# Layer 1 attention reordered: two q/k units at steps 4 and 6, the output projection in halves through the single bank, low parts a score tile later

## Chip, cores and metric

One core of one Trainium2 chip. The metric is the device time of one execution in microseconds. The kernel before took 2039.24 us in the median of 3 runs (2036.27 to 2040.58).

## What is computed

Two transformer-like layers on x of 8 batches x 512 tokens x 256 features, each layer being x + attention(layernorm(x)) + ffn(layernorm(x)). The change lies in layer 1's attention alone (16 heads of 16, a bias that depends on the distance of two positions):

```python
qkv = jnp.einsum('bsd,ed->bse', x, Wqkv); q, k, v = jnp.split(qkv, 3, axis=-1)
logits = jnp.einsum('bihd,bjhd->bhij', q, k) * scale + pos_bias[None]
attn = jax.nn.softmax(logits, axis=-1)
out = jnp.einsum('bhij,bjhd->bihd', attn, v).reshape(B, S, D)
return jnp.einsum('bsd,ed->bse', out, Wout)
```

## The kernel before

Layer 1's attention is `biased_attention` (L656 to L1188). All 8 batches run through one software pipeline. A batch has 32 steps (STEPS). Each step issues one score tile (L1118 on PE: two matmuls for two heads, 128 queries x 512 keys; on VectorE, L1042, two passes that add the bias and take the row maximum) and one probability tile (L1136 on PE, 128 keys x 512 queries for two heads), which belongs to a step 12 earlier (LAG). Of four probability tiles three are copied out of PSUM by ScalarE (L991) and get their bias from GpSimd (L950, through `add_bias` L831), and one (n % 4 == 1) gets it from VectorE straight out of PSUM (L1055). ScalarE takes the exponential three steps later (TAKEN, L994), and at every second step PE multiplies two exponentiated tiles with the values ("value", L1147) into o_bank.

High precision products are made of two parts of each operand: ScalarE writes a high part in fp32r, VectorE the rest (the "low part": L1033 for x, L1036 for q and k, L1040 for the mixed heads), and three matmuls of fp32r stand for one (PARTS, `product` L1087).

Everything else that a batch needs is placed at fixed steps (L732 to L751), some of it for the next batch (+1) and some for the last (-1): load and norm of x (x_load, ln_stats, ln_rstd, ln), its transposes (x_turn, steps 18 and 19), the four q/k units of the next batch ("qk", 22, 23, 28, 29: q and k for heads 0 to 7, then q and k for heads 8 to 15), the products for v (17), the transposed maxima ("maxima", 1, 9, 17, 25), the turn and norm of each head quad (heads_turn, heads_norm), the two turns of the last batch's mixed heads (mix_turn, 24 and 27) and its output projection and store ("out", "store", 31). "stack" (steps 27 and 28 for the next batch, 4 and 12 for this one) is six DMAs on SyncE's queue that copy q/k parts into the layout of the score tiles; it waits for both low parts of its half of the heads (L911). "maxima" puts two DMAs on the same queue (L925), and the first probability tile of a quad waits for them (L1141).

The order is one list for all engines (STEADY): for every step the placed events, then prob, prob_exp and score. Each engine walks it (`turns`, L791) and executes its own part in that order, with semaphores between. Turns -1, 0, 7 and 8 are written out; turns 1 to 6 are a hardware loop (L798).

PSUM: three slots of two banks hold the paired uses (score, prob, v, out) in turn; a use waits until the one three places earlier in the list has been read (`claim`, L1073). One single bank holds maxima, x_turn, qk, heads_turn and mix_turn, each waiting for VectorE's last read of the one before. o_bank holds the values' sum. In the opening batch x_turn and qk use the slots instead of the single bank (`bank`, L782).

```python
for s in range(STEPS):
    STEADY += placed[s]
    STEADY.append(("prob", 0 if s >= LAG else -1, (s - LAG) % STEPS))
    at = s - LAG - TAKEN
    STEADY.append(("prob_exp", 0 if at >= 0 else -1, at % STEPS))
    STEADY.append(("score", 0, s))
```

## Time and profile before

| what | value |
|---|---|
| median of 3 runs | 2039.24 us (2036.27 to 2040.58) |
| the profiled execution | 2048.42 us |
| its span, first to last instruction | 2046.7 us |
| mean granted clock of TensorE | 0.930 |
| busy over the span | PE 87%, PEld 56%, DVE 56%, ACT 52%, POOL 48% |
| layer 1 attention, scores | first 1195.37, last 1813.25 us from the start |

```profile
span 2046.7 us, 34076 instructions
...
PE   4988988887999999999996967878878778877999
PEld 3455555544788888888885733333334333326566
DVE  5666566662253353443433368767877877845435
ACT  2455555555532232232322228877877878885642
POOL 2344444432344444434432528766766767784202
PEclk7899999997999999999998959989889888988999
```

PE is TensorE's matmuls, PEld its weight loads, DVE is VectorE, ACT ScalarE, POOL GpSimd, SP SyncE. Each digit is the busy share of a fortieth of the span (51 us) in tenths; PEclk is the clock that was granted, in tenths of 2.4 GHz. Layer 1's attention fills slices 24 to 36. In the rows of a timeline the columns are: start in us, duration in us, engine, line, operation, output<-input, shape, how many instructions are merged, and in brackets the idle time before with the engine and tile that ended it. Matmuls overlap, so a merged row's duration runs to the end of its last one. A score tile on VectorE is two rows of L1049; L1089 is the matmul of `product`, whoever calls it; L835 is the addition of the bias.

### The profile page before, as it was taken

The numbers are of one execution on the slowest core, as the hardware profiler recorded it, in microseconds if no ns is written. First come the engines' busy times: TensorE is split into PE (matmuls) and PEld (weight loads), VectorE is DVE, ScalarE is ACT, GpSimd is POOL, SyncE is SP. The second block draws the span as 40 slices with busy tenths as digits, with TensorE's granted clock in tenths as the row PEclk, the third lists the DMA queues.
The fourth block names the chain that finished last, engine by engine and source line by source line (L and its number), as shares of the span: only waits on it lengthen the run. The fifth ranks groups of instructions, "written<-read, shape, count | busy, mean of one in ns | idle before, by whom it ended". The sixth has DMA issues, their size and how long they took to land. (4 is left out here: it accounts for less than half of the span.)

```text
span 2046.7 us, 34076 instructions
## 1 busy us (share of the span) xinstructions
PE 1773.9 (87%) x11015; PEld 1149.2 (56%) x11015; DVE 1150.4 (56%) x2519; ACT 1066.1 (52%) x1455; POOL 978.8 (48%) x736
## 2 busy tenths in 40 slices
PE   4988988887999999999996967878878778877999
PEld 3455555544788888888885733333334333326566
DVE  5666566662253353443433368767877877845435
ACT  2455555555532232232322228877877878885642
POOL 2344444432344444434432528766766767784202
PEclk7899999997999999999998959989889888988999
DMA  3333333324420121111201442222122222116456
GB/s 120 86 104 101 90 93 89 93 66 148 160 80 24 56 68 35 56 54 38 67 27 55 160 151 78 82 60 79 56 76 90 62 68 77 42 55 228 129 157 209
DMA packets 119261, 182.74 MB, mean 89 GB/s; under 512 B 14197, under 2 KB 73077, under 8 KB 119162
## 3 DMA queue, kind: packets, MB, share of 16 engines
q1 hardware_dynamic: 110076, 171.11, 27.4%
q10 hardware_dynamic: 8448, 8.39, 1.2%
q0 software_dynamic: 640, 2.10, 0.3%
q8 instruction: 42, 0.69, 0.1%
q14 instruction: 55, 0.45, 0.1%
HBM read 90.72 MB, written 39.91 MB: 64 GB/s over the span
## 5 line engine op out<-in xcount | busy, mean ns | idle before, releaser
L835 POOL TENSOR_TENSOR l_prob<-l_prob,l_bias 128x1024 f32<-128x1024 f32 x192 | 452.8, 2378 | 165.0 <-ACT l_prob L991 164.3
L1268 POOL TENSOR_TENSOR f_hl<-f_full,f_hh 128x512 fp32r<-128x512 f32 x192 | 248.4, 1294 | 410.3 <-DVE f_hh L1306 270.5
L1049 DVE CUSTOM_DVE_ANT_0 l_slot<-l_slot,l_bias 128x512 f32<-128x512 f32 x512 | 340.5, 715 | 73.0 <-PE l_slot L1128 62.9
L994 ACT ACTIVATE l_prob<-l_prob 128x1024 f32<-128x1024 f32 x256 | 270.9, 1070 | 0.0
L493 DVE TENSOR_REDUCE l_peak<-l_slot 128x2 f32<-128x256 f32 (+3 forms) x256 | 206.3, 822 | 108.8 <-PE l_slot L585 105.6
L1356 PE MATMUL f_ps<-f_hh,f_hi_h 128*128 128x512 f32 x1024 | 260.3, 390 | 3.4 <-ACT f_hh L1280 2.5
L1356 PE MATMUL f_ps<-f_hl,f_hi_h 128*128 128x512 f32 x1024 | 258.3, 389 | 0.0
L397 ACT ACTIVATE l_prob<-l_slot 128x1024 f32<-128x1024 f32 (+3 forms) x256 | 175.4, 706 | 100.8 <-PE l_slot L604 97.9
L991 ACT COPY l_prob<-l_slot 128x1024 f32<-128x1024 f32 x192 | 194.7, 1014 | 50.1 <-PE l_slot L1144 49.5
L1356 PEld LDWEIGHTS f_ps<-f_hh,f_hi_h 128*128 128x128 f32 x1024 | 192.0, 188 | 46.7 <-issue 3.2
L1356 PEld LDWEIGHTS f_ps<-f_hl,f_hi_h 128*128 128x128 f32 x1024 | 192.2, 188 | 39.9
L1288 ACT ACTIVATE f_full<-f_ps,f_h_s 128x512 f32<-128x512 f32 x128 | 87.0, 685 | 234.8 <-PE f_ps L1356 215.9
L336 POOL TENSOR_SCALAR_AFFINE_SELECT l_prob<-l_prob 128x256 f32<-128x256 f32 x256 | 106.1, 422 | 213.8 <-ACT l_prob L397 211.2
L1306 DVE CAST f_hh<-f_full 128x512 fp32r<-128x512 f32 x128 | 62.2, 486 | 256.2 <-ACT f_full L1288 256.2
L1128 PE MATMUL l_slot<-l_stacks 63*128 63x512 f32 x512 | 125.0, 488 | 61.5 <-DVE l_prob L835 27.4
L1158 PE MATMUL l_o_bank<-l_prob,l_vals 128*32 128x512 f32 x1024 | 155.3, 682 | 4.7 <-ACT l_prob L994 4.7
L1144 PE MATMUL l_slot<-l_stacks 64*128 64x512 f32 x512 | 138.3, 539 | 22.4 <-DVE l_peak L1049 16.2
L1144 PEld LDWEIGHTS l_slot<-l_stacks 64*128 64x128 f32 x512 | 52.8, 204 | 138.7 <-DVE l_peak L1049 85.1
L580 PE MATMUL l_slot<-l_stacks 63*128 63x256 f32 (+2 forms) x512 | 98.8, 383 | 29.8 <-ACT l_prob L397 16.4
L604 PE MATMUL l_slot<-l_stacks 64*128 64x256 f32 (+2 forms) x512 | 111.6, 435 | 11.3 <-DVE l_peak L493 4.1
L1128 PEld LDWEIGHTS l_slot<-l_stacks 63*128 63x128 f32 x512 | 54.4, 209 | 101.1 <-DVE l_prob L835 41.7
L618 PE MATMUL l_o_bank<-l_prob,l_vals 128*32 128x512 f32 (+3 forms) x1024 | 101.5, 470 | 9.9 <-POOL l_prob L336 8.7
(228 smaller groups left out, 2811.7 us busy)
## 6 DMA issues: line engine op xcount, KB each, us to landing
l_stacks<-l_parts SPq DMA_DIRECT2D x384, 128.0 KB, 2.6
attn<-l_out_sb ACTq DMA_DIRECT2D x16, 512.0 KB, 3.1
f_raw<-in_L_ffn_h_w SPq DMA_DIRECT2D x16, 512.0 KB, 4.1
f_raw<-in_L_ffn_h_w SPq DMA_DIRECT2D x32, 256.0 KB, 2.6
e_w<-in_L_ffn_f SPq DMA_DIRECT2D x32, 256.0 KB, 3.0
l_bias<-ext SPq DMA_DIRECT2D x16, 448.0 KB, 8.5
l_x_in<-in_L_attn_x SPq DMA_DIRECT2D x8, 512.0 KB, 3.9
xh<-l_xh SPq DMA_DIRECT2D x8, 512.0 KB, 2.6
```

Source lines behind the costliest of these rows:

```text
L397: act.activation(prob[:, n // 2 % RING, 2 * pr:2 * pr + 2, j * P:T], slot(kind, n)[:, :, j * P - q0:wide], ACT.Exp).then_inc(p_exp.sem, 1)
L493: dve.tensor_reduce(peak[:, g, :, pr, t], slot(kind, n)[:, :, 0:(t + 1) * P], AX_X, ALU.max)\
L604: ins = pe.matmul(out[:, a, 0:wide], stacks[r, 1, 2 * g + pr, j * P:(j + 1) * P], stacks[r, 0, 2 * g + pr, q0:T], start=True, stop=True)
L835: return eng.tensor_tensor(probs(n), src, bias[:, h:h + 2, j * P:j * P + T], ALU.add)
L991: act.copy(probs(n), slot(kind, n)[:]).then_inc(p_copied.sem, 1)
L994: act.activation(probs(n), probs(n), ACT.Exp).then_inc(p_exp.sem, 1)
L1049: ins = dve.tensor_tensor_reduce(src, src, bias[:, 4 * g + 2 * pr + a, t * P:t * P + T], 1.0, 3 * NEG, ALU.add, ALU.max, peak[:, g, a, pr, ...
L1128: ins = pe.matmul(out[:, a], stacks[r, 0, 2 * g + pr, t * P:(t + 1) * P], stacks[r, 1, 2 * g + pr, ::-1], start=True, stop=True)
L1144: ins = pe.matmul(out[:, a], stacks[r, 1, 2 * g + pr, j * P:(j + 1) * P], stacks[r, 0, 2 * g + pr, ::-1], start=True, stop=True)
L1158: ins = pe.matmul(o_bank[32 * a:32 * a + 32, :], vals_sb[:, v0:v0 + 32], prob[:, n % RING, a], start=(j == 0), stop=(j == TT - 1), skip_gr ...
L1268: pool.tensor_tensor(t.hl[layer % 2][:, o], t.full[:, n % 2], t.hh[layer % 2][:, o].bitcast(F32), ALU.subtract).then_inc(self.h_lo.sem, 1)
L1356: ins = pe.matmul(t.hidden[n % 4][:], t.hi[m][:, k, cut], src[layer % 2][:, k], start=first and k == 0, stop=last and k == KH - 1, skip_gr ...
```

## The change

The list of steps is changed, and with it what the single bank and the slots hold.

- q/k units 2 and 3 leave steps 28 and 29 of the batch before; they are computed in their own batch at steps 4 and 6. Unit 1 moves from step 23 to 24, mix_turn 0 from 24 to 23. Stack 2 moves from step 4 to 8.
- The low part of a q/k unit is an event of its own on VectorE, behind the score tile of the step instead of ahead of the additions and the score.
- The output projection is two events (steps 30 and 31) of 12 matmuls each into the single bank, each copied by ScalarE (512 columns); the store follows the second. It no longer takes a slot, so the list of paired uses has 65 entries instead of 66 and its ring of three starts anew at each batch: at the wrap the claim is two uses back instead of three (`claim` looks for the last use of the same slot).
- In the opening batch units 2 and 3 also go through the single bank, and the first score waits for two low parts instead of four.

```diff
--- before.py
+++ after.py
@@ -720,7 +720,7 @@
     value_ps, o_copied, ot_ps = sem("value_ps", QUADS * TT), sem("o_copied", QUADS), sem("ot_ps", QUADS)
     inv_ready, mix_ready = sem("inv_ready", QUADS), sem("mix_ready", QUADS)
     mt_ps, mh_ready, ml_ready = sem("mt_ps", KD), sem("mh_ready", KD), sem("ml_ready", KD)
-    out_ps, out_ready = sem("out_ps", 1), sem("out_ready", 1)
+    out_ps, out_ready = sem("out_ps", TT // 2), sem("out_ready", TT // 2)
     out_saved = sem("out_saved", 1, grant=1, unit=16)
     held_sp, held_dve = sem("held_sp"), sem("held_dve")
 
@@ -737,7 +737,7 @@
         placed[s].append(("heads_copy", off, g))
         off, s = later(8 * g + 9)
         placed[s].append(("maxima", off, g))
-        off, s = later((27, 28, 36, 44)[g] - STEPS)
+        off, s = later((27, 28, 40, 44)[g] - STEPS)
         placed[s].append(("stack", off, g))
     for g, s in enumerate((26, 34, 42, 52)):
         off, s = later(s)
@@ -745,23 +745,25 @@
     for s, *events in ((0, ("x_load", 1, 0)), (17, ("v", 0, 0)),
                        (3, ("ln_stats", 1, 0)), (4, ("ln_stats", 1, 1)), (5, ("ln_stats", 1, 2)),
                        (6, ("ln_stats", 1, 3), ("ln_rstd", 1, 0)), (8, ("ln", 1, 0)),
-                       (18, ("x_turn", 1, 0)), (19, ("x_turn", 1, 1)), (22, ("qk", 1, 0)), (23, ("qk", 1, 1)),
-                       (24, ("mix_turn", -1, 0)), (27, ("mix_turn", -1, 1)), (28, ("qk", 1, 2)), (29, ("qk", 1, 3)),
-                       (31, ("out", -1, 0), ("store", -1, 0))):
+                       (18, ("x_turn", 1, 0)), (19, ("x_turn", 1, 1)), (22, ("qk", 1, 0)), (24, ("qk", 1, 1)),
+                       (4, ("qk", 0, 2)), (6, ("qk", 0, 3)), (23, ("mix_turn", -1, 0)), (27, ("mix_turn", -1, 1)),
+                       (30, ("out", -1, 0)), (31, ("out", -1, 1), ("store", -1, 0))):
         placed[s] += events
     for s in range(STEPS):
         STEADY += placed[s]
+        lows = [("qk_low", off, n) for kind, off, n in placed[s] if kind == "qk"]
         STEADY.append(("prob", 0 if s >= LAG else -1, (s - LAG) % STEPS))
         at = s - LAG - TAKEN
         STEADY.append(("prob_exp", 0 if at >= 0 else -1, at % STEPS))
         STEADY.append(("score", 0, s))
+        STEADY += lows
 
 
     LAST_READ = {"score": a_max, "prob": None, "v": v_ready, "out": out_ready,
                  "maxima": tops_ready, "x_turn": xl_ready, "qk": low_ready, "heads_turn": mix_ready, "mix_turn": ml_ready}
-    PAIRED = [e for e in STEADY if e[0] in ("score", "prob", "v", "out")]
-    SINGLE = [e for e in STEADY if e[0] in ("maxima", "x_turn", "qk", "heads_turn", "mix_turn")]
-    assert len(PAIRED) % 3 == 0
+    PAIRED = [e for e in STEADY if e[0] in ("score", "prob", "v")]
+    SINGLE = [e for e in STEADY if e[0] in ("maxima", "x_turn", "qk", "heads_turn", "mix_turn", "out")]
+    assert len(PAIRED) % 3 != 1
 
     def pooled(n):
         return n % 4 != 1
@@ -781,9 +783,9 @@
 
     def bank(kind, n, b):
 
-        if not opening(b):
+        if not opening(b) or n >= 2:
             return single[:]
-        return slots[2][:, n] if kind == "x_turn" else slots[n // 2][:, n % 2]
+        return slots[2 if kind == "x_turn" else 0][:, n]
 
     def there(b):
         return not isinstance(b, int) or 0 <= b < B
@@ -1000,12 +1002,13 @@
                     wait(act, mt_ps, n + 1, b)
                     act.copy(mixt[:, 0, n], single[:]).then_inc(mh_ready.sem, 1)
                 if kind == "out":
-                    wait(act, out_saved, 1, b - 1)
-                    wait(act, out_ps, 1, b)
-                    act.copy(out_sb[:].rearrange("p (a t) d -> p a (t d)", a=2), slot(kind, 0)[:])\
+                    if n == 0:
+                        wait(act, out_saved, 1, b - 1)
+                    wait(act, out_ps, n + 1, b)
+                    act.copy(out_sb[:, 2 * n:2 * n + 2].rearrange("p t d -> p (t d)"), single[:])\
                        .then_inc(out_ready.sem, 1)
                 if kind == "store":
-                    wait(act, out_ready, 1, b)
+                    wait(act, out_ready, TT // 2, b)
                     act.dma_start(out_d[b].rearrange("(t p) d -> p t d", p=P), out_sb[:]).then_inc(out_saved.sem, 16)
             turns(act, emit)
 
@@ -1031,9 +1034,9 @@
                 if kind == "x_turn":
                     wait(dve, xh_ready, n + 1, b)
                     dve.tensor_tensor(xl[:, n], bank(kind, n, b), xh[:, n].bitcast(F32), ALU.subtract).then_inc(xl_ready.sem, 1)
-                if kind == "qk":
+                if kind == "qk_low":
                     wait(dve, high_ready, n + 1, b)
-                    dve.tensor_tensor(parts[:, n // 2, n % 2 * 3], bank(kind, n, b), parts[:, n // 2, 1 + n % 2].bitcast(F32),
+                    dve.tensor_tensor(parts[:, n // 2, n % 2 * 3], bank("qk", n, b), parts[:, n // 2, 1 + n % 2].bitcast(F32),
                                       ALU.subtract).then_inc(low_ready.sem, 1)
                 if kind == "mix_turn":
                     wait(dve, mh_ready, n + 1, b)
@@ -1073,7 +1076,9 @@
             def claim(uses, depth, kind, n, i):
 
                 at = [(u[0], u[2]) for u in uses].index((kind, n))
-                for m in range(at - depth, at - len(uses) - 1, -depth):
+                for m in range(at - 1, at - len(uses) - 1, -1):
+                    if m % len(uses) % depth != at % depth:
+                        continue
                     before, off, k = uses[m]
                     bb = i + off - (1 if m < 0 else 0)
                     if there(bb):
@@ -1100,7 +1105,7 @@
                 if kind == "qk":
                     if opening(b):
                         pe.wait_ge(w_ready.sem, 2)
-                    else:
+                    if not opening(b) or n >= 2:
                         claim(SINGLE, 1, kind, n, i)
                     weight, cut = (wk if n % 2 else wq), slice(n // 2 * P, (n // 2 + 1) * P)
                     wait(pe, xl_ready, KD, b)
@@ -1119,7 +1124,7 @@
 
                     g, pr, t = score_of(n)
                     if n == 0 and opening(b):
-                        wait(pe, low_ready, 4, b)
+                        wait(pe, low_ready, 2, b)
                     out = claim_pair(kind, n, i)
                     if n % 8 == 0:
                         wait(pe, stack_in[g], 6, b)
@@ -1175,10 +1180,10 @@
                 if kind == "out":
                     if opening(b):
                         pe.wait_ge(w_ready.sem, 4)
-                    out = claim_pair(kind, n, i)
+                    claim(SINGLE, 1, kind, n, i)
                     wait(pe, ml_ready, KD, b)
-                    for t in range(TT):
-                        ins = product(out[:, t // 2, (t % 2) * D:(t % 2 + 1) * D],
+                    for t in range(2 * n, 2 * n + 2):
+                        ins = product(single[:, (t % 2) * D:(t % 2 + 1) * D],
                                       [(mixt[:, q, k, t * P:(t + 1) * P], wo[:, p, k]) for k in range(KD)
                                        for p, q in PARTS])
                     ins.then_inc(out_ps.sem, 1)
```

## Rows read from the trace of the kernel before

**Rows 1.** Busy us by stretch: length, PE, PEld, DVE, ACT, POOL, clock, DMA.
```profile
1505.00:1587.00 82.00, 65.05 (x364) 29.87 (x364) 61.99 (x167) 63.83 (x75) 57.80 (x26) 0.90 0.25 71
```
**Rows 2.** Timeline of VectorE where one batch follows another.
```profile
1504.66 0.70 DVE L1049 CUSTOM_DVE_ANT_0 l_slot<-l_slot,l_bias 128x512 f32<-128x512 f32 x1 [3.01 <-PE l_slot L1128]
...
1582.11 0.70 DVE L1049 CUSTOM_DVE_ANT_0 l_slot<-l_slot,l_bias 128x512 f32<-128x512 f32 x1 [4.36 <-PE l_slot L1128]
...
1586.94 0.70 DVE L1049 CUSTOM_DVE_ANT_0 l_slot<-l_slot,l_bias 128x512 f32<-128x512 f32 x1 [3.43 <-PE l_slot L1128]
...
1749.71 0.70 DVE L1049 CUSTOM_DVE_ANT_0 l_slot<-l_slot,l_bias 128x512 f32<-128x512 f32 x1 [1.09 <-PE l_slot L1128]
```
**Rows 3.** Timeline of PE and VectorE, steps 21 to 25.
```profile
1553.81 0.69 DVE L1049 CUSTOM_DVE_ANT_0 l_slot<-l_slot,l_bias 128x512 f32<-128x512 f32 x1
...
1554.52 0.40 PE L1128 MATMUL l_slot<-l_stacks 63*128 63x512 f32 x2
...
1555.07 0.68 DVE L1036 TENSOR_TENSOR l_parts<-l_single,l_parts 128x512 fp32r<-128x512 f32 x1
...
1555.67 0.69 DVE L1049 CUSTOM_DVE_ANT_0 l_slot<-l_slot,l_bias 128x512 f32<-128x512 f32 x1
...
1555.85 0.50 PE L1089 MATMUL l_single<-l_xl,l_wk 128*128 128x512 f32 x1
...
1557.42 0.50 PE L1144 MATMUL l_slot<-l_stacks 64*128 64x512 f32 x2
...
1558.15 0.69 DVE L1036 TENSOR_TENSOR l_parts<-l_single,l_parts 128x512 fp32r<-128x512 f32 x1 [1.08 <-ACT l_parts L978]
...
1558.89 0.66 PE L1173 MATMUL l_single<-l_ident,l_mix 128*128 128x128 f32 x4 [0.73 <-DVE l_parts L1036]
...
1561.24 0.28 PE L1134 MATMUL l_single<-l_ident,l_peak 128*16 128x128 f32 x1
...
1563.69 0.68 DVE L1049 CUSTOM_DVE_ANT_0 l_slot<-l_slot,l_bias 128x512 f32<-128x512 f32 x1
```
**Rows 4.** Timeline of PE and VectorE, steps 27 to 31.
```profile
1567.62 0.69 DVE L1049 CUSTOM_DVE_ANT_0 l_slot<-l_slot,l_bias 128x512 f32<-128x512 f32 x1
...
1573.92 1.22 DVE L835 TENSOR_TENSOR l_prob<-l_slot,l_bias 128x1024 f32<-128x1024 f32 x1
...
1575.05 0.69 DVE L1049 CUSTOM_DVE_ANT_0 l_slot<-l_slot,l_bias 128x512 f32<-128x512 f32 x1
...
1575.62 1.06 PE L1158 MATMUL l_o_bank<-l_prob,l_vals 128*32 128x512 f32 x8
...
1576.62 4.63 PE L1089 MATMUL l_slot<-l_wo,l_mixt 128*128 128x256 f32 x24
...
1581.51 0.40 PE L1128 MATMUL l_slot<-l_stacks 63*128 63x512 f32 x2
```
**Rows 5.** Busy time by stretch, for PE's granted clock (PEclk).
```profile
1522.60:1532.80 10.20, 7.78 (x32) 3.08 (x28) 6.41 (x17) 8.18 (x11) 6.75 (x4) 0.52 0.02 3
...
1540.80:1543.90 3.10, 3.10 (x30) 2.94 (x26) 0.28 (x3) 1.28 (x2) 3.10 (x2) 1.00 0.12 46
...
1573.80:1577.20 3.40, 2.01 (x13) 0.93 (x14) 3.40 (x9) 2.30 (x3) 1.98 (x1) 0.95 0.54 166
...
1576.60:1581.20 4.60, 4.60 (x30) 4.45 (x26) 1.15 (x4) 0.00 (x0) 1.00 (x1) 0.63 0.00 0
```
**Rows 6.** Busy time by stretch, S4 to S8.
```profile
1513.49:1521.79 8.30, 5.19 (x33) 1.83 (x33) 8.19 (x27) 6.43 (x7) 6.92 (x4) 1.00 0.31 81
```
**Rows 7.** Timeline of SyncE's queue in batch 0.
```profile
1210.19 1.47 SPq L925 DMA_DIRECT2D l_stacks<-l_tops  x2
```
**Rows 8.** Timeline of the end of the attention.
```profile
1845.50 0.63 PE L1173 MATMUL l_single<-l_ident,l_mix 128*128 128x128 f32 x4 [0.90 <-DVE l_mix L1065]
...
1846.78 0.69 DVE L1040 TENSOR_TENSOR l_mixt<-l_single,l_mixt 128x512 fp32r<-128x512 f32 x1 [1.43 <-ACT l_mixt L1001]
...
1854.74 1.01 ACT L1005 COPY l_out_sb<-l_slot 128x1024 f32<-128x1024 f32 x1 [5.47 <-PE l_slot L1089]
```

## Prediction

> **What bounds the kernel now.** I name the score, probability and value tiles S0 to S31, P0 to P31 and V0 to V15; a step issues one S and one P. First view: busy time by stretch. Over one batch of layer 1 attention (82 us) PE is busy 79%, VectorE 76%, ScalarE 78%, GpSimd 70% [rows 1]. No engine is full, so the batch is bound by hand-overs, and the question is where VectorE (which must start an S each step) sits idle. Second view: VectorE's timeline. S0 starts at 1504.66 and at 1586.94, so a batch takes 82.3 us; S31 comes at 1582.11 (VectorE idle 4.36 before it), and S0 follows 4.83 us after S31 [rows 2]. Third view: the same timeline around steps 22 to 31, where two q/k units and the output projection stand. PE runs in order with three paired PSUM slots: anything long put before P and S starves VectorE directly, and a user of the single bank waits until VectorE has read the one before.
>
> **Part 1, steps 22 to 25: low parts later, a mix turn in between.** Per batch the same work, in another order. Before, low 0 starts right after S21 (1555.07), qk1's product runs on PE from 1555.85 to 1557.42 (1.57 us), low 1 follows at 1558.15 after 1.08 us idle, the maxima turn is issued at 1561.24 and S25 starts at 1563.69 [rows 3]. Durations: S takes 1.26 (1553.81 to 1555.07), a low part 0.60 (to 1555.67) and PE goes on 0.74 after its start (1558.15 to 1558.89); PE hands S to VectorE 0.60 after its issue (1581.51 to 1582.11); a mix turn's low part starts 1.28 after the turn (1845.50 to 1846.78) [rows 2, 3, 4, 8].
> Now the new order, from the unchanged issue of S22 at 1554.52. S22 starts at 1555.12, low 0 at 1556.39, and PE gets the bank for the mix turn at 1557.13 (before, qk1 had it at 1555.85). Its low part starts at 1558.41, so S23 at 1559.01, and PE may start qk1 at 1559.15; after 1.57 come P12 and, 0.34 later, S24, issued at 1561.06, started at 1561.66. Low 1 starts at 1562.93. The maxima turn waits for it until 1563.67, 2.4 us later than before; P13 follows 0.2 later, addition 13 starts at 1564.47 and takes 1.13, S25 starts at 1565.60. Cost: 1565.60 - 1563.69 = **+1.91 us**. The chain through the single bank is the path, and each low part behind a score lengthens it by that score. Behind the maxima turn on PE are queued P13, S25 and the heads turn, and VectorE waits for them. Bound from below: +0.6, one low part, if tiles issued ahead covered the rest; from above +2.5, two whole scores. I stay with the chain, since the old rows show no slack in it.
>
> **Part 2, steps 27 to 29: qk2 and qk3 gone.** S27 to S29 took 1575.05 - 1567.62 = 7.43 us: two products of 1.57, each followed by a low part with some 1.1 us of idle before it (as the 1.08 in rows 3), and addition 17, 1.13 until the next starts (1573.92 to 1575.05) [rows 3, 4]. Without them: S27 1.27, S28 1.27 and the addition 1.13 follow without a gap, 3.68 with rounding. Cost: **-3.75 us**. What is late next is ScalarE's copy of P16; it frees S29's slot at about the end of addition 17, so it hides. GpSimd's additions run in 3 of 4 steps and their exponentials are read three steps later: covered. Bound from the other side: -1.5, if only the two idles go and ScalarE's copies set the steps.
>
> **Part 3, the output projection in halves.** Before: 24 matmuls from 1576.62, 4.63 us, then ScalarE's copy of 1.01 us (as in rows 8), the store and only then P19's copy [rows 4]. S29 to S31 is 1582.11 - 1575.05 = 7.06. The size of a half depends on the granted clock. In the projection's stretch it averages 0.63, against 1.00 in the stretch of v, where 24 matmuls of the same width take 3.1 us [rows 5]. The clock fell to 1.2 GHz right after a stretch in which PE was busy 2.01 of 3.40 us, because S29's slot was held by P17 until addition 17 was done [rows 4, 5]. In the new order S29 waits only about 0.2 us, and V5, P17, S29 and half 0 stand close together, so I take 2.4 GHz: 1.52 us a half. Counting from S29 at 0: S30 at 1.32 (VectorE hardly waits), then V6 (1.0), half 1, P19, S31: S31 at 4.50. So 4.50 - 7.06 = **-2.56 us**. At 1.2 GHz (2.3 a half) S31 comes at 6.0, so -1.07: the weak end. ScalarE makes two copies of half the width instead of one of 1.01, some +0.2, beside PE's work. The first half's copy needs the bank only until half 1, which waits for V6 anyway.
>
> **Part 4, the edge of the loop.** The pair list has 65 uses instead of 66, so at the wrap P20 waits for P19's copy and S0 for S31, two uses back instead of three. S0 would be ready some 2.5 us after S31's start: 1.5 until its slot is free, 0.34 for the issue, 0.60 for the hand-over. But where the loop branches VectorE starts S0 4.83 us after S31 and has been idle 3.43, while on leaving the loop it was idle 1.09 only [rows 2]. The difference is the loop's own, and it covers the shorter distance: **0**. If that cover is gone (the entry to batch 1, which does not branch) it costs 0.8 once. By the Trainium skill (Runtime: NRT & Kernel Launch, Instruction fetch mechanics) a taken branch to a page not held forces a fetch before execution goes on. By the row and by this rule the sum is the same; the rule says from where the gap counts, which rival C turns on, and the trace agrees as far as 3.43 us against 1.09 go.
>
> **Part 5, steps 4 to 8: qk2 and qk3 put in.** S4 to S8 is 1521.79 - 1513.49 = 8.30 us, with addition 25 and the norm's statistics between, and VectorE is busy for 8.19 of them [rows 6]. Hence two low parts cost 1.2 fully: nothing below that. The first product also comes before P24 and S4 on PE: 1.57 us, of which PE was about 1 us ahead of VectorE, so S4 comes 0.6 later. The second starts when low 2 is done and ends inside S5 and the statistics. **+1.85** with rounding. Upper end: both products bare, 2 x (1.6 + 0.6) = 4.4. SyncE: stack 2 (six DMAs, 4 us of its queue) moves from step 4 to just behind low 3, ahead of the maxima's two; in a steady batch two steps lie between and S16 is far away: 0.
>
> **Batches.** 1 to 6 have it all: 1.91 - 3.75 - 2.56 + 1.85 = -2.55, times 6 = -15.3. Batch 7 has no next q/k: +1.85, and its projection, which runs at the high clock already, gains about a third of part 3, 0.8: +1.05. Batch 0: score-only steps with PE at 1.2 GHz, a product 2.6 us (6 x 512 columns): S4 comes 1.25 later, low 2 adds 0.6, the second product 1.3 and low 3 0.6: S7 comes 3.75 later, and the maxima's DMAs (issued at 1210.19 [rows 7], P0 waits for them) now queue behind stack 2's, another 1.2: +4.9 by S12; at steps 22 to 31 it has no mix turn and no projection: +1.0 (half of part 1), -3.3 (part 2, where GpSimd is nearer to full), +0.8 (part 4): -1.5. So +3.4. The tail: half 1 waits for half 0's copy, 1.0, less the 0.4 that the last copy of 1.01 us [rows 8] shrinks, and 0.3 for the higher clock's share: +0.3. New idle on PE at steps 22 to 25 (some 1.3, 0.8 and 1.2 us) may drop the clock; I take one spell in three batches at 1.2 us each: +2.4.
> Sum: -15.3 + 1.05 + 3.4 + 0.3 + 2.4 = **-8.15 us**. The profiled run took 2048.42 (span 2046.7, 1.7 outside it), 9.2 above the median of 2039.24; I set the sum against the former (2040.3), and carried to the median it is **2031.1**.
>
> **Rivals.**
> A, slower: the single bank's convoy lowers the clock. For it: between 1555.85 and 1564.5 the new order leaves PE 62% busy; stretches at 60% (2.01 of 3.40, rows 5) came before a fall. Against: the old stretches there are dense and at 1.00. Price: qk1's product +1.0, V3 +0.9, two thirds on the path, +1.3; and the halves stay at 1.2 GHz. Per batch 1.91 + 1.3 - 3.75 - 1.07 + 1.85 = +0.24; with 3.4 + 1.05 + 0.3 = 4.75 for batches 0, 7 and the tail +6.2: 2045.4. It decides from a net of -0.1 us per batch up. The Trainium skill (TensorE: Matmul & The Clock Gate, A second HAM failure mode: psum-queue depth-cycling) speaks for this one: short PE idles between groups while cycling PSUM made the clock oscillate. The trace agrees at one place: the fall at 1577.2 came after such a wait.
> B, no change: only the projection stays at 1.2 GHz. Net -1.06 per batch: -6.4 + 4.75 = -1.6, so 2037.6.
> C, much faster: PE's 10.2 us at a clock of 0.52 after S8 [rows 5] go too, since PE is busier at steps 4 to 7. PE is busy 7.78 of them, which would be some 3.7 less at full clock, two thirds of it on the path: 2.4 a batch, seven times: 2014.3. Against: ScalarE's norm still holds P28 and PE idles there as before. If instead the loop's gap ran from earlier than S31, five edges would give 2 us each: 2021.
> D: that the change doesn't do what it says. The order is written out, so only the clock can undo it.
>
> **How the numbers follow.** Forecast 0.50, A 0.22, B 0.16, C 0.12. A measurement of this kernel tells 0.2% (4.1 us) from nothing. The forecast alone spans 2025 to 2038 (part 5 at 2.5, part 1 at 2.5, or the clock's 2.4 gone), so a seventh of it lies within 0.2%. Range 2017 to 2047: both ends leave out half of C and the outer quarter of A. Faster 0.51, same 0.24, slower 0.25.
>
> **What would show it.** S0 to S0 near 79.7 us in batches 1 to 6. S24 to S26 later by 2 us with PE waiting for VectorE's low part before the maxima turn; no idle of 4.36 before S31; two groups of 12 matmuls of about 1.5 us; two low parts between S4 and S7. Batch 0 longer by 3 us. Wrong if the projection's halves take 2.3 us (A or B), if a clock below 1.00 stands in steps 22 to 25 (A), if P20 or S0 waits for ScalarE's copy with VectorE idle past 4.8 us (part 4), or if VectorE idles between S4 and S8 (part 5 too small).

## The result and the profile after

| | before | after |
|---|---|---|
| median of the runs, us | 2039.24 (2034.96 to 2045.96) | 2023.15 (2018.14 to 2023.84, 5 runs) |
| ratio to before | 1 | 0.9908, 95% interval 0.988 to 0.9937 |
| profiled execution: its time, its span | 2048.42, 2046.7 | 2022.3, 2020.6 |
| mean granted clock | 0.930 | 0.948 |

The change makes the kernel 16.1 us faster at the medians, where 8.15 had been forecast (2031.1); 2023.15 lies inside the range. The two profiled executions are 26.1 us apart. Not all of that is the change's: S0 of batch 0 starts 4.7 us earlier already (1190.69 against 1195.37), in stages that the change doesn't touch, while from the attention's first transpose to S0 it is 17.4 us before and 17.3 after. From S0 of batch 0 to S31 of batch 7 it is 617.27 us before and 593.24 after: 24.0 less, by the same steps in each batch. These traces are therefore compared step by step, and times by the medians.

The first view is busy time by stretch, batches 3 to 5 after (S0 to S0, as in [rows 1]; columns: stretch, PE, PEld, VectorE, ScalarE, GpSimd busy, granted clock, DMA share, GB/s):

```profile
1410.00:1488.66 78.66, 61.46 (x364) 27.28 (x364) 61.87 (x166) 63.86 (x76) 57.69 (x26) 0.96 0.26 74
1488.66:1567.41 78.75, 61.52 (x364) 27.51 (x364) 61.88 (x166) 63.90 (x76) 57.73 (x26) 0.96 0.25 74
1567.41:1645.97 78.56, 61.42 (x364) 27.78 (x364) 61.89 (x167) 63.75 (x76) 57.63 (x26) 0.96 0.25 74
```

VectorE, ScalarE and GpSimd do the same 62, 64 and 58 us of work as before; PE's 65.05 fell to 61.5, by its clock alone (0.90 to 0.96). The batch is 78.7 us instead of 82, so 3.3 us of waiting and slow PE went. It is still bound by hand-overs: no engine is over 82% busy.

The second view is the timeline of steps 22 to 25, where the low parts and the mix turn moved (as in [rows 3]; columns: start, duration, engine, line, operation, tiles, count, idle before and its releaser):

```profile
1538.95 0.70 DVE L1052 CUSTOM_DVE_ANT_0 l_slot<-l_slot,l_bias 128x512 f32<-128x512 f32 x1
...
1540.21 0.69 DVE L1039 TENSOR_TENSOR l_parts<-l_single,l_parts 128x512 fp32r<-128x512 f32 x1
...
1540.95 0.66 PE L1178 MATMUL l_single<-l_ident,l_mix 128*128 128x128 f32 x4 [1.21 <-DVE l_parts L1039]
...
1543.01 0.50 PE L1094 MATMUL l_single<-l_xl,l_wk 128*128 128x512 f32 x1 [0.73 <-DVE l_mixt L1043]
...
1545.54 0.70 DVE L1052 CUSTOM_DVE_ANT_0 l_slot<-l_slot,l_bias 128x512 f32<-128x512 f32 x1 [1.26 <-PE l_slot L1133]
...
1549.51 0.69 DVE L1052 CUSTOM_DVE_ANT_0 l_slot<-l_slot,l_bias 128x512 f32<-128x512 f32 x1
```

S22, low 0 behind it at 1540.21, the mix turn (PE idle 1.21 for that low part), qk1 (idle 0.73 for the mix turn's low part), S24, S25: the chain that part 1 wrote down. The third view is the same timeline from step 29 on (as in [rows 4]):

```profile
1556.07 1.70 PE L1094 MATMUL l_single<-l_wo,l_mixt 128*128 128x256 f32 x12
...
1557.14 0.69 DVE L1052 CUSTOM_DVE_ANT_0 l_slot<-l_slot,l_bias 128x512 f32<-128x512 f32 x1
...
1557.86 0.59 ACT L1008 COPY l_out_sb<-l_single 128x512 f32<-128x512 f32 x1 [0.37 <-PE l_single L1094]
...
1559.36 1.69 PE L1094 MATMUL l_single<-l_wo,l_mixt 128*128 128x256 f32 x12
...
1561.91 0.70 DVE L1052 CUSTOM_DVE_ANT_0 l_slot<-l_slot,l_bias 128x512 f32<-128x512 f32 x1 [1.87 <-PE l_slot L1133]
...
1563.72 0.40 PE L1133 MATMUL l_slot<-l_stacks 63*128 63x512 f32 x2
...
1567.41 0.70 DVE L1052 CUSTOM_DVE_ANT_0 l_slot<-l_slot,l_bias 128x512 f32<-128x512 f32 x1 [4.10 <-issue]
```

The idle before S31 is 1.87 instead of 4.36, and the halves take 1.70 and 1.69 each. But PE had issued S0's last products at 1563.72, and VectorE began S0 only at 1567.41, after 4.10 us in which it waited for nothing that the profile shows. That gap was 3.43 before [rows 2]. The sequencer's records for VectorE (DVEq) show the loop's branch and the next instruction behind it. After (line, name, operation, count, shortest/median/longest ns, first and last start):

```profile
L800 DVEq COMPARE_BRANCH  x1: 63/63/63, 1562.5 to 1562.5; - x1
...
L800 DVEq FUSED_REGOPS  x1: 67/67/67, 1567.1 to 1567.1; - x1
```

And before:

```profile
L798 DVEq COMPARE_BRANCH  x1: 63/63/63, 1582.7 to 1582.7; - x1
...
L798 DVEq FUSED_REGOPS  x1: 67/67/67, 1586.7 to 1586.7; - x1
```

The branch comes 0.6 us behind S31's start in both; from it to the next instruction it is 4.6 us after and 4.0 before.

The steps from S(n) to S(n+1), mean of batches 1 to 5 of each trace:

| stretch | before | after | difference | forecast |
|---|---|---|---|---|
| S21 to S25 (part 1) | 9.88 | 11.88 | +2.0 | +1.91 |
| S27 to S29 (part 2) | 7.43 | 3.69 | -3.74 | -3.75 |
| S29 to S31 (part 3) | 6.75 | 4.77 | -2.0 | -2.56 |
| S31 to S0, S0 to S1 (part 4) | 4.57, 3.46 | 5.45, 2.60 | +0.9, -0.9 | 0 |
| S2 to S8 (part 5) | 11.82 | 12.86 | +1.0 | +1.85 |
| S8 to S12 | 11.31 | 10.74 | -0.6 | 0 |
| S0 to S0 | 81.73 | 78.54 | -3.2 | -2.55, and a clock reserve of 0.4 |

Batch 6 gained more (81.95 to 75.34): no branch back follows it, and its clock was low for 21.7 us before and 6.8 after. Batches 1 to 6 gave 22.6 us together.

### The profile page after: what moved, and what is told of

The parts are those of the page before. It is cut to its first block and busy times, and to the rows that moved or that the text cites. A ratio compares the mean times of both kernels' runs of the same rounds, so it can differ in the third digit from the quotient of the medians.

```text
span 2020.6 us, 34092 instructions
## 1 busy us (share of the span) xinstructions
PE 1743.3 (86%) x11015; PEld 1136.4 (56%) x11015; DVE 1147.6 (57%) x2519; ACT 1066.8 (53%) x1463; POOL 978.9 (48%) x736
## 5 line engine op out<-in xcount | busy, mean ns | idle before, releaser
L1149 PE MATMUL l_slot<-l_stacks 64*128 64x512 f32 x512 | 132.2, 515 | 28.3 <-ACT l_prob L993 12.4
L1163 PE MATMUL l_o_bank<-l_prob,l_vals 128*32 128x512 f32 x1024 | 145.7, 643 | 6.0 <-ACT l_prob L996 6.0
L1133 PE MATMUL l_slot<-l_stacks 63*128 63x512 f32 x512 | 116.5, 457 | 35.9 <-ACT l_prob L993 17.1
L604 PE MATMUL l_slot<-l_stacks 64*128 64x256 f32 (+2 forms) x512 | 110.0, 429 | 11.3 <-DVE l_peak L493 4.1
L1281 ACT ACTIVATE f_tanh<-f_ps,f_gate_s 128x512 f32<-128x512 f32 x64 | 44.0, 688 | 122.3 <-PE f_ps L1331 122.1
```

The lines of the kernel that those rows point to most:

```text
L604: ins = pe.matmul(out[:, a, 0:wide], stacks[r, 1, 2 * g + pr, j * P:(j + 1) * P], stacks[r, 0, 2 * g + pr, q0:T], start=True, stop=True)
L1133: ins = pe.matmul(out[:, a], stacks[r, 0, 2 * g + pr, t * P:(t + 1) * P], stacks[r, 1, 2 * g + pr, ::-1], start=True, stop=True)
L1149: ins = pe.matmul(out[:, a], stacks[r, 1, 2 * g + pr, j * P:(j + 1) * P], stacks[r, 0, 2 * g + pr, ::-1], start=True, stop=True)
L1163: ins = pe.matmul(o_bank[32 * a:32 * a + 32, :], vals_sb[:, v0:v0 + 32], prob[:, n % RING, a], start=(j == 0), stop=(j == TT - 1), skip_gr ...
```

## The experiments

**Theory 1** after this reading: the sum by parts holds, and the late low parts are its one loss. **Rival**: the gain comes from the order of steps as a whole, or from PE's clock (17.1 us of the 81.7 at 1.2 GHz before, 6.8 of 78.5 after). A second theory came up with the third view: at the loop's edge VectorE has a stall of its own that takes back part of what the halves give. The kernels of one group shared their runs of the kernel before: medians 2044.05 (the first four), 2038.88 (the next four) and 2040.84 (the last), so ratios are what to compare.

### The low parts at once

```diff
         lows = [("qk_low", off, n) for kind, off, n in placed[s] if kind == "qk"]
+        STEADY += lows
...
         STEADY.append(("score", 0, s))
-        STEADY += lows
```

> The changed kernel with one part undone: a q/k unit's low part stands again ahead of the additions and the score of its step. Theory 1 (each part acts by the hand-over it moves, and the late low parts cost by lengthening the chain through the single bank): S21 to S25, 9.6 us before and 11.8 after the change in its trace, comes back by 1.0 to 2.0 us a batch, S4 to S8 stays within 0.4 us, and the time falls by 6 to 14 us below the changed kernel's 2023: 2009 to 2017. Theory 2 (the change gained by TensorE's clock, the order of low parts does not matter): within 3 us of 2023.

Measured: 2015.78 us (2012.0 to 2020.1), ratio 0.9865 (0.9838 to 0.9892), so 0.0043 or some 9 us under the change's 0.9908; the two intervals overlap a little, so the steps have to say where it comes from. S21 to S25 falls from 11.88 to 9.83 (before: 9.88): the late low parts of qk0 and qk1 cost 2.0 us a batch. S2 to S8 rises from 12.86 to 13.56, but that is the clock and not the low parts: batch 1, with no low clock in this stretch, takes 12.06 here and 12.07 in the change, and batches 2 to 4, with 4.0 us of it, take 14.3. At steps 4 to 6 it makes no difference whether the low parts are late (S4 to S8 is 0.6 shorter at once, step 3 is 0.6 longer). S8 to S12 rises by 0.5, with the low clock too, and so a batch falls by 0.7 only (78.54 to 77.85). In batch 0 step 11 takes 1.55 again instead of 2.67. So the change contains a loss of 2.0 us a batch, of which this run gives back 0.7 net, and Theory 1 stands: the clock was low for longer than in the change, and the kernel was faster.

### qk2 and qk3 back at steps 28 and 29

```diff
-                       (4, ("qk", 0, 2)), (6, ("qk", 0, 3)), (23, ("mix_turn", -1, 0)), (27, ("mix_turn", -1, 1)),
+                       (28, ("qk", 1, 2)), (29, ("qk", 1, 3)), (23, ("mix_turn", -1, 0)), (27, ("mix_turn", -1, 1)),
```

> The changed kernel with q/k units 2 and 3 back at steps 28 and 29 of the batch before, low parts still late. Theory 1: S27 to S29 takes again 7 to 9 us instead of 3.7, S4 to S8 falls by about 1 us, together +2.5 to +4.5 a batch over 7 batches: 2041 to 2054. Theory 2 (the clock did it): the time follows the time at 1.2 GHz per batch, 6.8 us in the changed kernel and 17.1 before; if that stays at 7 the kernel stays below 2030.

Measured: 2087.6 us, ratio 1.021 (1.018 to 1.024): a miss, and the slowest kernel of the study. S27 to S29 takes 8.01 (3.69 in the change) and S29 to S31 9.13 (4.77). PE's timeline in batch 2 of this kernel:

```profile
1418.96 0.50 PE L1094 MATMUL l_single<-l_xl,l_wk 128*128 128x512 f32 x1 [1.21 <-DVE l_parts L1039]
...
1424.30 2.93 PE L1094 MATMUL l_single<-l_wo,l_mixt 128*128 128x256 f32 x12 [3.02 <-DVE l_parts L1039]
...
1428.82 1.69 PE L1094 MATMUL l_single<-l_wo,l_mixt 128*128 128x256 f32 x12
```

PE stands for 3.02 us because the first half needs the single bank, which qk3's low part frees only behind a score; then that half runs at 1.2 GHz and takes 2.93. The time in the low clock grows to 14 to 28 us a batch. This is Rival A's convoy, with two more units in it than the change has: late low parts, and a projection that queues for the same bank. Moving qk2 and qk3 away is therefore not one saving among others but what the other two moves need: in this setting it is worth 9.8 us a batch (88.33 against 78.54), the low clock that comes with it included, where parts 2 and 5 of the prediction together gave 1.9.

### The projection whole again

```diff
-                       (30, ("out", -1, 0)), (31, ("out", -1, 1), ("store", -1, 0))):
+                       (31, ("out", -1, 0), ("store", -1, 0))):
...
-    SINGLE = [e for e in STEADY if e[0] in ("maxima", "x_turn", "qk", "heads_turn", "mix_turn", "out")]
+    SINGLE = [e for e in STEADY if e[0] in ("maxima", "x_turn", "qk", "heads_turn", "mix_turn")]
...
-                    for t in range(2 * n, 2 * n + 2):
-                        ins = product(single[:, (t % 2) * D:(t % 2 + 1) * D],
+                    for t in range(TT):
+                        ins = product(out[:, t // 2, (t % 2) * D:(t % 2 + 1) * D],
```

> The changed kernel with the output projection whole again: 24 matmuls at step 31 into a paired slot, one copy. Theory 1: VectorE idles 3 to 4.4 us before S31 again, S29 to S31 back from 4.8 to 6 to 7 us, +1 to +2 us a batch over 7: 2030 to 2038. Rival: the halves gained nothing of their own and S0, held by the loop's edge, takes up the delay: within 3 us of 2023.

Measured: 2027.99 us, ratio 0.9925 (0.9899 to 0.9951), between the two expectations, and by the intervals not told apart from the change's 0.9908. S29 to S31 is 5.56 (4.77 in halves), so the halves gain 0.8 there, but S31 to S0 is 4.54 (5.45 in halves): S29 to S0 is 10.10 whole and 10.22 in halves. What the halves win, VectorE gives back at the loop's edge. They keep it only where no branch back follows: from S29 to the next S0 batch 6 takes 7.0 against 8.1, and S29 to S31 of batch 7 takes 4.6 against 5.4. (Batch 0 is 1.6 us shorter in the change too, but no projection runs in it, so that isn't the halves'.)

### PE's idle stretch filled, in the kernel before

```diff
-                    for a in range(2):
+                    for a in tuple(range(2)) * {7: 4, 8: 3}.get(n, 1):
                         r = head(a, HROWS - 1)
```

The products are done again into the same place, so the output is the same.

> The kernel before, with the matmuls of S7 issued four times and of S8 three times into the same slots (same result), 1.7 us more work per batch in PE's idle time ahead of the stretch of 10.2 us at 1.2 GHz after S8. Theory 2 (clock): that stretch vanishes, S9 to S12 takes 1.5 to 2.5 us less and the kernel gains 10 to 18 us: 2021 to 2029. Theory 1 (hand-overs): the stretch at 1.2 GHz may go, but it is off the path: within 5 us of 2039.

Measured: 2052.46 us (2043.65 to 2065.91), ratio 1.0041 (1.0018 to 1.0064). The stretch at 1.2 GHz did not vanish, it became irregular:

```profile
1339.11:1424.85 85.74, 68.39 (x374) 30.74 (x374) 63.66 (x167) 63.88 (x76) 57.70 (x26) 0.86 0.23 68
1505.77:1586.09 80.32, 64.10 (x370) 28.85 (x370) 62.15 (x167) 63.42 (x75) 57.37 (x26) 0.92 0.25 73
```

23.9 us at 1.2 GHz in the first of these batches, 12.1 in the second; over batches 1 to 5 it is 15.0 a batch, against 16.9 before. As a test of whether the low stretch after S8 costs Rival C's 2.4 us it is inconclusive, since the clock wasn't changed as meant. What it shows is that matmuls added to keep PE busy need not keep the clock up: two batches had more time at the low level than any before.

### The loop written out, after and before

```diff
-        turn(-1)
-        turn(0)
-        with eng.Fori(1, B - 1) as i:
-            turn(i)
-        turn(B - 1)
-        turn(B)
+        for i in range(-1, B + 1):
+            turn(i)
```

> The changed kernel with its hardware loop over batches 1 to 6 written out; nothing else. Theory 3 (VectorE's gap at the loop's edge is the jump's own, and it swallows what the halves gain between S29 and S31): S31 to S0 falls from 5.4 to about 2.2 us at all five edges, as where the loop is left today; batches 1 to 5 take 75.3 instead of 78.6: -16 us, 2003 to 2010. Rival (the gap comes from the claims two uses back, or from PE or ScalarE, not from the jump): the gap stays, within 4 us of 2023.

Measured: 2003.9 us (2001.11 to 2006.09), ratio 0.982 (0.9803 to 0.9836), as Theory 3 expected. The same edit in the kernel before:

> The kernel before with its loop over batches 1 to 6 written out. Theory 3: S31 to S0 from 4.6 to 2.5 us, S0 to S1 from 3.5 to 2.9, 2.7 us at each of five edges: -11 to -16 us, so a ratio of 0.992 to 0.995 to the kernel before. And the distance between the two unrolled kernels is larger than between the two with a loop, by about 1 us for each of five edges. Rival: no change.

Measured: 2026.03 us, ratio 0.9936 (0.9921 to 0.9952), as expected. VectorE's timeline at S31 and S0 of the change written out:

```profile
1555.62 0.70 DVE L1048 CUSTOM_DVE_ANT_0 l_slot<-l_slot,l_bias 128x512 f32<-128x512 f32 x1 [1.87 <-PE l_slot L1129]
...
1557.81 0.70 DVE L1048 CUSTOM_DVE_ANT_0 l_slot<-l_slot,l_bias 128x512 f32<-128x512 f32 x1 [0.79 <-PE l_slot L1129]
```

And of the kernel before written out:

```profile
1559.55 0.70 DVE L1045 CUSTOM_DVE_ANT_0 l_slot<-l_slot,l_bias 128x512 f32<-128x512 f32 x1 [2.71 <-PE l_slot L1124]
...
1561.99 0.70 DVE L1045 CUSTOM_DVE_ANT_0 l_slot<-l_slot,l_bias 128x512 f32<-128x512 f32 x1 [1.04 <-PE l_slot L1124]
```

The idle before S0 is 0.79 instead of 4.10, and 1.04 instead of 3.43. A batch falls from 78.54 to 75.01 with the change, at the same 6.8 us of low clock, and from 81.73 to 78.21 in the kernel before. The second pair holds more than the branch: the low clock fell from 17 to 10 us a batch there, and the profiled execution (2017.1) was the fastest of seven. By the medians it is 12.9 us, 2.6 for each of five branches. Without an edge the change is worth 1 - 0.982 / 0.9936 = 1.2%, with it 0.9%, a difference that the intervals don't tell from nothing.

### The projection whole, written out

The two edits of the last sections together.

> The changed kernel with layer 1's loop over the batches written out, and the output projection whole (12 products into a pair bank at step 31) in place of the two halves. With the loop the whole projection cost 4.8 us (2027.99 against 2023.15), although steps 29 and 30 were 0.8 us longer per batch, because VectorE's gap at the loop's edge was 0.9 us shorter. Theory 1 (the edge swallows the halves' gain): without edges, all eight batches pay what the edgeless ones paid with the loop, 1.2 to 1.6 us each, 9.6 to 12.8 in all: 2013 to 2017 us beside 2003.9 of the written-out halves, with the mean of S29 to S0 over 1.0 us longer. Rival (the halves bring the same with or without an edge, some 0.6 us a batch): 2007 to 2010.

Measured: 2019.95 us (2016.59 to 2024.03), ratio 0.9895 (0.9871 to 0.9919), against 0.982 in halves: 0.0075, or 15 us, as far apart as Theory 1 had said or a little more (2013 to 2017 was expected), and past its rival. (The expectation had counted batch 0 among those that paid; it has no projection.) S29 to S0 is 7.85 whole and 6.81 in halves: 1.0 us a batch with nothing to take it back. The other 0.7 of the 1.7 a batch (76.72 against 75.01) stands mostly in steps 0 to 3, in the batches with most time at 1.2 GHz: the batches with 3.4 us at the low clock take 75.6, those with 13.7 take 78.0 and 78.2.

```profile
1410.50:1486.10 75.60, 60.24 (x368) 27.30 (x372) 61.68 (x166) 63.43 (x75) 57.51 (x26) 0.98 0.26 77
1486.10:1564.20 78.10, 63.84 (x369) 28.34 (x372) 61.96 (x167) 63.63 (x75) 57.63 (x26) 0.91 0.26 76
```

So the edge hid what the halves are worth: by the steps from S29 to S0 -0.1 us a batch with the branch and 1.0 without. In the ratio it is 0.0017 and 0.0075, the second with the clock's part in it.

### Late low parts for qk2 and qk3 alone

```diff
         lows = [("qk_low", off, n) for kind, off, n in placed[s] if kind == "qk"]
+        STEADY += [e for e in lows if e[2] < 2]
...
         STEADY.append(("score", 0, s))
-        STEADY += lows
+        STEADY += [e for e in lows if e[2] >= 2]
```

> The changed kernel with late low parts only for units 2 and 3 (steps 4 and 6), those of units 0 and 1 (steps 22 and 24) at once. Theory 1: S21 to S25 as in the run with all low parts at once (9.8 us instead of 11.9), S2 to S8 as in the changed kernel (12.9 instead of 13.6): -2.0 a batch against the changed kernel over seven, 2007 to 2013. Rival (the two places compensate, the single bank's chain only moves): as the run with all low parts at once, ratio 0.9865 or above.

Measured: 2021.97 us (2016.87 to 2026.22), ratio 0.9914 (0.9896 to 0.9931): no better than the change, a miss. S21 to S25 is 9.83 as expected. S2 to S8 is 13.41 and not the change's 12.86 (12.07 in batch 1 of both; 14.35 here where 4.1 us of it are at 1.2 GHz), and the time at 1.2 GHz grew from batch to batch:

```profile
1256.47:1332.60 76.13, 64.12 (x377) 28.26 (x369) 61.26 (x166) 65.91 (x79) 60.58 (x27) 0.93 0.28 82
1486.50:1565.00 78.50, 64.84 (x364) 28.98 (x364) 61.43 (x167) 63.76 (x76) 57.70 (x26) 0.89 0.26 74
```

10.2 us low in the first of these batches, 17.1 in the second, in the same code: 2.4 us of time beside 6.9 us more at the low clock (1.9 against the batch between, 76.50 with 10.1 low). The expectation had left the clock as it was in the change (6.8 a batch), and that was its error.

### The same, with the loop written out

> Both: late low parts only at steps 4 and 6, and the loop written out. If the two gains add: 14 us from late low parts and 16 from the edges below the changed kernel, 1990 to 1998, a ratio near 0.978 to the kernel before. If the clock or ScalarE (64 us of work in a batch of 72) takes one of them back: 1999 to 2008.

Measured: 1987.1 us (1985.8 to 1991.05), ratio 0.9743 (0.9725 to 0.9761), below the 1990 of the forecast: the fastest kernel here, 2.6% under the kernel before and, by the ratios, 1.7% under the change. Two kinds of batch remain:

```profile
1323.06:1395.44 72.38, 59.62 (x368) 27.10 (x371) 61.48 (x166) 63.53 (x76) 57.62 (x26) 0.98 0.28 81
1395.44:1469.26 73.82, 63.50 (x368) 28.31 (x371) 61.44 (x167) 63.55 (x76) 57.65 (x26) 0.91 0.27 80
```

3.4 us at 1.2 GHz in the first, 13.7 in the second: 1.4 us of time for 10.3 us. Here 0.14 us of time go with each microsecond of low clock, in the kernel above some 0.3.

## Why the prediction was right, step by step

The direction and the range held, and the likeliest case came true in its mechanism. The size was off by 8 us at the medians. The measured 2023.15 lies nearer to Rival C's 2021 than to the forecast, but by the number alone: neither of C's two mechanisms showed at its price. In the traces, the change's own part from batch 0 to the attention's end is -24.3 (-22.6 in batches 1 to 6, -1.15 in batch 0, -0.55 in batch 7 and the tail) against -8.15 forecast; the medians, 16.1 apart, say that an average pair of executions differs by less than this one.

**Part 1** (+1.91): +2.0. The single bank's chain, each low part a score later, was right, and the first experiment gives it back alone. PE's new waits of 1.21 and 0.73 for the low parts stand where the working put them, and the clock reserve of 2.4, kept for them, was not needed.

**Part 2** (-3.75): -3.74. But the prediction priced the removal as independent of the rest. The experiment that put qk2 and qk3 back measured 88.33 us a batch: in the new order their place is worth 9.8 us. From before to after the steps give it 2.7 (3.74 less the 1.04 of part 5); no run moved them alone in the old order.

**Part 3** (-2.56): -2.0 in its own stretch. The halves ran at 2.4 GHz, as taken, in 1.7 instead of 1.52 us each, which makes S29 to S31 4.77 and not 4.50. The other 0.3 is on the side of before: the batch of the rows took 7.06 there, the mean of five 6.75. S31 waits 1.87 for PE and not 4.36.

**Part 4** (0): 0 in the sum of S31 to S0 (+0.9) and S0 to S1 (-0.9), which is luck: two gaps changed, and the prediction had neither. It took the loop's gap as it was, counted from S31, and so let part 3's gain pass the edge in full. Counting from S31 was right: VectorE's branch is recorded 0.6 us behind S31's start at all 35 loop edges of the seven kernels with a loop. In the kernel with qk2 and qk3 back S31 lies 3.3 us behind S30 at three edges and 4.2 at two, and S0 follows S31 by 5.3 us at all five. Rival C's anchor ahead of S31 is therefore wrong. What failed is the length: from the branch to VectorE's next instruction it is 4.4 to 4.6 us in the four looped kernels with halves (the change, low parts at once, low parts split, qk2 and qk3 back), and 3.5 to 4.0 in the three others (before, before with the stretch filled, projection whole). The other engines go on 0.2 to 0.3 us behind their branch.

The records of the DMA engines say more. At each of these edges two transfers of instructions of 8 KB follow VectorE's branch, and S0 starts 2.1 to 2.2 us behind the start of the second; the written-out kernels have none between S31 and S0. The first starts 0.6 to 0.9 us behind the branch in the kernels with the shorter gap, and 1.2 to 1.6 in those with the longer. What else differs there is the output's store of 512 KB, which ScalarE issues 0.1 us ahead of S31 in the kernels with halves and 0.4 behind it in the others. The store on ScalarE's queue, after and before:

```profile
1561.83 0.38 ACTq L1012 DMA_DIRECT2D attn<-l_out_sb  x1
...
1582.51 0.38 ACTq L1009 DMA_DIRECT2D attn<-l_out_sb  x1
```

The store is 528 transfers. With halves 295 to 470 of them start before the first transfer of instructions and all before the second; in the others it is 0 to 68 and 278 to 465. That the store delays the instructions fits all seven kernels, but no run moved the store, so it isn't shown. The -0.9 of S0 to S1 is a gap of its own: before, VectorE waits another 0.6 to 0.9 us between S0 and addition 21 for nothing that the profile shows, and with the change not at all. It waits there in the kernel before filled and in the one with qk2 and qk3 back too, and not in the other four; why is open.

By the Trainium skill (Runtime: NRT & Kernel Launch, Instruction fetch mechanics) a taken branch to a page not held forces a fetch before execution goes on. The traces agree with it: the two transfers stand behind the branch, and in the two written-out kernels, without one, 3.3 and 2.1 us of S31 to S0 go.

**Part 5** (+1.85, "nothing below" 1.2): +1.0, the step whose bound failed. The two low parts do cost 0.6 each (steps 4 and 6), and step 3 grew by 0.5, but step 7 lost 0.6 that the prediction had not seen. (Step 3 grew only behind a branch: in batch 1 and in the written-out kernel it takes 1.59, as before.) The loss of step 7 lies in one small operation of the norm. VectorE's and GpSimd's timeline of the kernel before:

```profile
1519.48 4.68 POOL L835 TENSOR_TENSOR l_prob<-l_prob,l_bias 128x1024 f32<-128x1024 f32 x2
...
1521.06 0.81 DVE L1029 SCALAR_TENSOR_TENSOR l_shift<-l_moments,l_rstd 128x4 f32<-128x4 f32 x1
```

And after:

```profile
1503.92 4.68 POOL L837 TENSOR_TENSOR l_prob<-l_prob,l_bias 128x1024 f32<-128x1024 f32 x2
...
1506.06 0.25 DVE L1032 SCALAR_TENSOR_TENSOR l_shift<-l_moments,l_rstd 128x4 f32<-128x4 f32 x1
```

The shift on four columns takes 0.81 us before and 0.25 after, and both end 0.05 us after the first of GpSimd's two additions (half of 4.68 us each: 1521.82 and 1506.26). It is so in six batches of either trace. In batch 0, where GpSimd has no addition, it takes 0.15. The window of S4 to S8 [rows 6] counted that wait as VectorE's busy time, "busy for 8.19 of them", and so hid 0.6 us of slack. The shift in batch 0 after, and the window of S4 to S8 after (columns as in the first view):

```profile
1204.84 0.15 DVE L1032 SCALAR_TENSOR_TENSOR l_shift<-l_moments,l_rstd 128x4 f32<-128x4 f32 x1
...
1497.32:1506.23 8.91, 6.20 (x38) 2.50 (x30) 8.79 (x28) 7.03 (x8) 6.52 (x4) 1.00 0.00 0
```

S4 to S8 grew by 0.61 only (8.91 against 8.30). The Trainium skill (SBUF — State Buffer, Who interferes with whom) says that a VectorE instruction with two SBUF inputs contends with a GpSimd instruction that reads SBUF, and that the shared ports are an exclusive lock. The traces agree, with the three durations above; no experiment tried it by itself.

**Batch 0** (+3.4): -1.15. S3 to S7 cost 1.6 where 3.75 were forecast: the first product took 2.9 us, at 1.2 GHz as forecast, the second 1.8, and steps 4 to 6 grew by 0.6, 0.4 and 0.6, so little more than the low parts showed. The maxima's DMAs behind stack 2 were right (+1.13 at step 11, forecast 1.2): they are issued 16.9 us after S0 and no longer 14.8, as SyncE's queue shows against [rows 7]:

```profile
1203.69 3.87 SPq L920 DMA_DIRECT2D l_stacks<-l_parts  x6
1207.61 1.47 SPq L927 DMA_DIRECT2D l_stacks<-l_tops  x2
```

Steps 21 to 31 gave 2.4, not 1.5. **Batch 7 and the tail** (+1.35): -0.55. Both last halves did run at 1.2 GHz (2.90 and 2.93 us), but the last copy ended 42.9 us after S31, against 43.1 before.

**The clock** (reserve +2.4): the other way. It fell for 6.8 us a batch and not 17.1, and S8 to S12 became 0.6 shorter, 3 us over these five batches. Rival C priced the end of the stretch of 10.2 us at 2.4 a batch; most of it did go, and gave a quarter of that. The price can be read across kernels: S8 to S12 takes 10.6 to 10.7 us in the batches of the change, low parts at once, split and projection whole that have 3.4 us of low clock there, and 11.3 to 11.5 in those with 9.6 to 10.7. C's price took two thirds of PE's slow time to be on the path. That less of it is because PE waits for ScalarE's norm there was not tested. Rival A was wrong for this order; its convoy came in the one with qk2 and qk3 left in place. Rival B fell with the halves' 1.7 us.

So of the 16 us difference between forecast and traces, 7.3 are batches 1 to 6 (0.6 in each of 1 to 5, from part 5 with 0.8 and the clock with 0.6, against 0.6 less from part 3 and smaller differences; in batch 6, where the most lies, 4.1), 4.6 batch 0, 1.9 batch 7 with the tail, and 2.4 the reserve.

## What to carry to other kernels

Operations that share one buffer are priced together: each unit put behind a score, and each new user of the bank, lengthens all those queued there, and the same two units, put back into the new order, cost 9.8 us a batch where the steps from before to after had given 2.7. A gain just ahead of a loop's edge should not be booked in full before the edge's own gap is looked at: here the gap behind the branch grew by as much as the halves won, and they paid only with the loop written out. Its length is not a constant of the loop, so look what else is under way when the branch comes. An operation whose duration is far above that of the same shape elsewhere is a wait in disguise, and should not be counted as busy when slack is bounded.

## What the hardware showed that was not expected

- The loop's branch cost VectorE 3.5 us a batch in the change (78.54 against 75.01 written out, at the same low clock). Most lies at S31 to S0 (5.45 against 2.20); 0.8 more lies between S2 and S8 (12.86 against 12.02). PE, ScalarE, GpSimd and SyncE went on 0.2 to 0.3 us behind theirs.
- VectorE's gap behind the same branch was 3.5 to 4.0 us in three kernels and 4.4 to 4.6 in four, and S0 started 2.1 to 2.2 us behind the second transfer of instructions at each of the 35 edges.
- The clock of PE settles into patterns over batches of the same code: changing between 3.4 and 13.7 us at 1.2 GHz a batch in two of the kernels, growing from 10.2 to 17.1 in another, constant at 6.8 in the change. With a microsecond at the low clock went 0.14 to some 0.3 us of the batch, within one kernel each time. With the low parts at once the clock was low for 17.1 us in three of six batches and for 10 to 14 in the others, and the kernel was still faster than the change.
- A VectorE operation on 128x4 takes 0.15, 0.25 or 0.81 us, by when GpSimd's addition beside it ends.
